# A mixture-of-experts block without a combining stage: residual rows stored early, weighted results added to them by scatters

## The reference, cut to what matters

```python
x = x + gnn(layernorm(x), edges)             # 6250 rows of 256, 200000 edges, 8 heads of 32
xt = layernorm(x)                            # input of the expert layer
probs = softmax(xt @ Wr + br)                # 8 experts
top_p, top_idx = top_k(probs, 2)
weights = top_p / top_p.sum(-1)              # the two weights of a token
xn = (xt - mean(xt)) * rsqrt(var(xt) + eps)
h = gelu((xn * ln_g[e] + ln_b[e]) @ W1[e] + b1[e])     # 256 -> 1024, for every expert e
y = h @ W2[e] + b2[e]                                  # 1024 -> 256
out = x + sum over the two chosen experts of weight * y
```

## Time and profile before

| what | us |
|---|---|
| median of 3 runs | 3188.27 (3187.75 to 3189.39) |
| the profiled execution: its own time | 3191.06 |
| the profiled execution: its span | 3189.4 |
| busy in the span: PE, DVE, ACT, POOL | 2071.1, 1937.4, 861.3, 1775.1 |

### The profile page before, as it was taken

The page is one execution under the profiler, slowest core; times in us unless marked ns, Lnnn a source line. Parts: engine busy times, 40 slices in busy tenths (PEclk is TensorE's granted clock), DMA queues, the critical chain, the costliest instruction groups (busy, mean ns, idle before and its releaser), DMA issues. The chain is left out here.

```text
span 3189.4 us, 46614 instructions
## 1 busy us (share of the span) xinstructions
PE 2071.1 (65%) x12432; PEld 1745.7 (55%) x12433; DVE 1937.4 (61%) x5386; ACT 861.3 (27%) x2271; POOL 1775.1 (56%) x1829
## 2 busy tenths in 40 slices
PE   3775666666666666666666666665342999999990
PEld 2444444444444444444444444444332999999980
DVE  6545666666666666666666666666783665656655
ACT  1222222222221112222222221111441555555540
POOL 1006777777777777777777777775475222212110
PEclk7997887878888888888878787777555999999995
DMA  1333444444444444444444444443444222212117
GB/s 44 112 110 101 109 108 108 109 108 108 109 108 108 109 108 108 109 108 108 109 108 108 109 108 108 109 108 83 136 138 137 66 79 64 86 56 73 41 43 241
DMA packets 192452, 327.35 MB, mean 103 GB/s; under 512 B 70287, under 2 KB 124542, under 8 KB 192428
## 3 DMA queue, kind: packets, MB, share of 16 engines
q0 software_dynamic: 98560, 256.53, 29.4%
q1 hardware_dynamic: 74328, 51.16, 5.7%
q10 hardware_dynamic: 19540, 19.40, 1.9%
HBM read 278.03 MB, written 47.99 MB: 102 GB/s over the span
## 5 line engine op out<-in xcount | busy, mean ns | idle before, releaser
L620 POOL DMA_INDIRECT rows<-proj_table,idx x1568 | 1486.3, 948 | 711.1 <-issue 418.2
L665 PE MATMUL banks<-weighed,onehot 128*128 128x264 f32 x3136 | 1082.8, 504 | 740.3 <-DVE weighed L736 739.5
L665 PEld LDWEIGHTS banks<-weighed,onehot 128*128 128x128 f32 x3136 | 735.5, 246 | 913.9 <-issue 767.6
L840 ACT ACTIVATE banks<-score,neg_bound 128x32 f32<-128x32 f32 x392 | 114.1, 291 | 1572.5 <-DVE score L729 1572.5
L726 DVE TENSOR_TENSOR raw_score<-rows,target 128x32 f32<-128x32 f32 x392 | 75.3, 192 | 717.4 <-DMA rows<-proj_table,idx 715.2
L736 DVE TENSOR_TENSOR weighed<-rows,banks 128x1024 f32<-128x1024 f32 x392 | 473.6, 1208 | 0.0
L1456 POOL DMA_INDIRECT results_by_token<-yrow,goes_to x104 | 108.9, 1047 | 478.6 <-DVE yrow L1404 350.4
L1343 ACT ACTIVATE hid<-banks,params 128x256 f32<-128x256 f32 x416 | 198.1, 478 | 267.7 <-PE banks L1299 261.1
L702 DVE TENSOR_TENSOR onehot<-banks,key_tab 128x512 f32<-128x512 f32 x397 | 270.1, 681 | 0.0
L1392 DVE TENSOR_TENSOR hidl<-hid,hidh 128x256 fp32r<-128x256 f32 x416 | 169.8, 424 | 149.7 <-ACT hidh L1337 149.5
L1299 PE MATMUL banks<-f_xth,w1h 128*128 128x256 f32 x832 | 236.4, 284 | 28.0 <-ACT hid L1343 14.5
(11 more groups left out here) (235 smaller groups left out, 2871.5 us busy)
## 6 DMA issues: line engine op xcount, KB each, us to landing
rows<-proj_table,idx POOLq DMA_INDIRECT x1568
w_raw<-in_L_ffn_W_dram POOLq DMA_DIRECT2D x16, 1024.0 KB, 6.3
xrow<-tokens_by_expert SPq DMA_DIRECT2D x106, 128.5 KB, 2.1
c_y<-results_by_token SPq DMA_DIRECT2D x10, 1120.0 KB
proj_table<-trow ACTq DMA_DIRECT2D x50, 128.9 KB
xin<-in_x_dram SPq DMA_DIRECT2D x50, 125.0 KB
skip_rows<-srow ACTq DMA_DIRECT2D x50, 125.0 KB
r_skin<-skip_rows SPq DMA_DIRECT2D x10, 625.0 KB
```

Source lines behind the costliest of these rows:

```text
L620: nc.gpsimd.indirect_dma_start(rows[k][:, i, :], None, table, bass.IndirectOffsetOnAxis(ap=idx[pair][:, col:col + 1], axis=0)).then_inc(ga ...
L665: mm = nc.tensor.matmul(acc_bank[u // 2 % 2][:, 0:ROW], onehot[u][:, i, :], weighed[:, k * SET + i, :], start=(u % 2 == 0 and i == 0), sto ...
```

## The change

The combining stage is dropped. While it routes, ScalarE's queue stores each chunk's x1 rows to the output. The weights are made chunk by chunk: ScalarE takes the exponential of the chunk's gaps, VectorE makes both shares and spreads them over 8 columns, one for each expert (0 where the token doesn't go). A row of `tokens_by_expert` now has 256 values, the token's number, and these 8 shares, so that one copy of a token serves both of its scatters: `second_copy` is gone. The scatters of the routing stage have 128 rows instead of 125; GpSimd first fills the 3 spare partitions with row numbers of dump rows and zeros. The loads of `r_skin` and `r_xin` are cut into parts of 112 and 13 partitions. In the expert stage VectorE copies the expert's column of shares, adds the bias into `biased`, multiplies by the share into `yrow`, and GpSimd's scatters wait for that (`y_shared`), go to the output itself, add there to what it holds, and leave out row numbers from 6250 on (padding). The diff, without declarations of semaphores and without the body of `combine_phase`:

```diff
-XROW = D + 1
+XROW = D + 1 + NX
-    xg = nc.dram_tensor("tokens_by_expert", (NX * CAP, XROW), F32).ap()
-    y2 = nc.dram_tensor("results_by_token", (2 * N + P, D), F32).ap()
+    xg = nc.dram_tensor("tokens_by_expert", (NX * CAP + P, XROW), F32).ap()
...
-            gaps=sb("gaps", [NP, NT]), warm=[sb(f"warm{k}", [P, 1]) for k in range(3)], weights=sb("weights", [NP, NT, 2]),
-            result_row=sb("result_row", [NP, NT, 2]), counts=sb("counts", [1, NX, 4], I32),
+            warm=[sb(f"warm{k}", [P, 1]) for k in range(3)],
+            result_row=sb("result_row", [NP, NT]), counts=sb("counts", [1, NX, 4], I32),
...
-        route_phase(nc, m, bank, x, skip_rows, xg)
-        expert_phase(nc, m, bank, xg, y2, ln_g, ln_b, W1, b1, W2, b2)
-        combine_phase(nc, m, y2, out)
+        route_phase(nc, m, bank, x, skip_rows, xg, out)
+        expert_phase(nc, m, bank, xg, out, ln_g, ln_b, W1, b1, W2, b2)
...
-            nc.gpsimd.iota(m["result_row"][:], [[2 * NP, NT], [1, 2]], base=0, channel_multiplier=2,
+            nc.gpsimd.iota(m["result_row"][:], [[NP, NT]], base=0, channel_multiplier=1,
...
+        SPARE = NP // 32 * 32
...
-        xn = [sb(f"r_xn{b}", [NP, C, 2, XROW]) for b in range(2)]
+        xn = [sb(f"r_xn{b}", [P, C, XROW]) for b in range(2)]
...
-        slot = [sb(f"slot{b}", [NP, C * 2], I32) for b in range(2)]
+        slot = [sb(f"slot{b}", [P, C * 2], I32) for b in range(2)]
...
+        gaps, shares, given = sb("gaps", [NP, C]), sb("shares", [NP, C, 2]), sb("given", [NP, C, 2, NX])
...
-                sp.dma_start(skin[c % 2][:], chunk(skip_rows, c)).then_inc(skin_loaded[c % 2], 16)
+                for part in NODE_PARTS:
+                    sp.dma_start(skin[c % 2][part], chunk(skip_rows, c)[part]).then_inc(skin_loaded[c % 2], 16)
...
-                sp.dma_start(xin[c % 2][:], chunk(x, c)).then_inc(xin_loaded[c % 2], 16)
+                for part in NODE_PARTS:
+                    sp.dma_start(xin[c % 2][part], chunk(x, c)[part]).then_inc(xin_loaded[c % 2], 16)
...
-                dve.wait_ge(skin_loaded[b], 16 * (c // 2 + 1))
+                dve.wait_ge(skin_loaded[b], 16 * len(NODE_PARTS) * (c // 2 + 1))
                 nc.vector.tensor_tensor(att[:], att[:], skin[b][:], ALU.add).then_inc(skin_used, 1)
+                if c == 0:
+                    dve.wait_ge(cleared, 4)
                 dve.wait_ge(skin_used, c + 1)
-                dve.wait_ge(xin_loaded[b], 16 * (c // 2 + 1))
+                dve.wait_ge(xin_loaded[b], 16 * len(NODE_PARTS) * (c // 2 + 1))
                 nc.vector.scalar_tensor_tensor(positive[:], att[:], 0.0, xin[b][:], ALU.max, ALU.add).then_inc(x_used, 1)
...
-                step(nc.vector.tensor_tensor(m["gaps"][:, of(c)], top8[:, :, 1], top8[:, :, 0], ALU.subtract))
-                dve.wait_ge(dve_step, steps[0] - 1)
+                nc.vector.tensor_tensor(gaps[:], top8[:, :, 1], top8[:, :, 0], ALU.subtract).then_inc(gaps_ready, 1)
+                settle()
                 if c:
-                    dve.wait_ge(slot_ready, 2 * c)
+                    dve.wait_ge(slot_ready, 3 * c)
...
                     dve.wait_ge(sent[b], 16 * 2 * C * (c // 2))
-                nc.vector.scalar_tensor_tensor(slot[b][:].rearrange("p (u k) -> p u k", k=2), pick[:], float(CAP), place[:],
+                nc.vector.scalar_tensor_tensor(slot[b][0:NP].rearrange("p (u k) -> p u k", k=2), pick[:], float(CAP), place[:],
                                                ALU.mult, ALU.add).then_inc(slot_ready, 1)
-                nc.vector.tensor_copy(xn[b][:, :, :, D], m["result_row"][:, of(c), :]).then_inc(slot_ready, 1)
+                dve.wait_ge(gaps_exp, c + 1)
+                step(nc.vector.tensor_scalar(shares[:, :, 1], gaps[:], 1.0, None, ALU.add))
+                settle()
+                step(nc.vector.reciprocal(shares[:, :, 0], shares[:, :, 1]))
+                settle()
+                step(nc.vector.tensor_tensor(shares[:, :, 1], shares[:, :, 0], gaps[:], ALU.mult))
+                settle()
+                step(nc.vector.tensor_tensor(given[:], one[:], shares[:].unsqueeze(3).to_broadcast([NP, C, 2, NX]), ALU.mult))
+                settle()
+                nc.vector.tensor_tensor(xn[b][0:NP, :, D + 1:XROW], given[:, :, 0, :], given[:, :, 1, :], ALU.add
+                                        ).then_inc(slot_ready, 1)
+                nc.vector.tensor_copy(xn[b][0:NP, :, D], m["result_row"][:, of(c)]).then_inc(slot_ready, 1)
...
             def second_norm(c):
                 for u in range(C):
                     t = c * C + u
-                    nc.vector.tensor_scalar(xn[c % 2][:, u, 0, 0:D], x1_of(t), mv[:, t, 0:1], rstd12[:, t:t + 1],
-                                            ALU.subtract, ALU.mult).then_inc(xn_first, 1)
+                    nc.vector.tensor_scalar(xn[c % 2][0:NP, u, 0:D], x1_of(t), mv[:, t, 0:1], rstd12[:, t:t + 1],
+                                            ALU.subtract, ALU.mult).then_inc(xn_ready, 1)
...
-            step(nc.vector.memset(padding[:, :, 0:D], 0.0))
+            step(nc.vector.memset(padding[:], 0.0))
+            settle()
             for h in range(FILL // P):
-                step(nc.vector.tensor_scalar(padding[:, h, D:XROW], m["iota_p"][:], float(2 * N), None, ALU.add))
+                step(nc.vector.tensor_scalar(padding[:, h, D:D + 1], m["iota_p"][:], float(N), None, ALU.add))
...
-            dve.wait_ge(weight_exp, 1)
-            then(nc.vector.tensor_scalar(wtmp[:], m["gaps"][:], 1.0, None, ALU.add))
-            then(nc.vector.reciprocal(m["weights"][:, :, 0], wtmp[:]))
-            then(nc.vector.tensor_tensor(m["weights"][:, :, 1], m["weights"][:, :, 0], m["gaps"][:], ALU.mult))
...
+            def gap_exponential(c):
+                act.wait_ge(gaps_ready, c + 1)
+                nc.scalar.activation(gaps[:], gaps[:], ACT.Exp).then_inc(gaps_exp, 1)
...
-            def second_copy(c):
-                act.wait_ge(xn_first, C * (c + 1))
-                nc.scalar.copy(xn[c % 2][:, :, 1, 0:D], xn[c % 2][:, :, 0, 0:D]).then_inc(xn_ready, 1)
+            def store_residual(c):
+                act.wait_ge(xn_ready, C * (c + 1))
+                rows = out[c * C * NP:(c + 1) * C * NP, :].rearrange("(u p) d -> p u d", u=C)
+                for part in NODE_PARTS:
+                    act.dma_start(rows[part], m["acc"][part, of(c), 0:D]).then_inc(x1_stored, 16)
...
             for c in range(CHUNKS):
                 if c + 1 < CHUNKS:
                     exponential(c + 1)
+                gap_exponential(c)
+                if c + 1 < CHUNKS:
                     deviations(c + 1)
-                second_copy(c)
+                store_residual(c)
                 if c + 1 < CHUNKS:
                     copy_turned(c + 1)
-            act.wait_ge(count_ready, 1)
-            nc.scalar.activation(m["gaps"][:], m["gaps"][:], ACT.Exp).then_inc(weight_exp, 1)
+            act.wait_ge(x1_stored, 16 * len(NODE_PARTS) * CHUNKS)
...
-            pe.wait_ge(slot_ready, 2 * CHUNKS)
+            pe.wait_ge(slot_ready, 3 * CHUNKS)
...
+            for b in range(2):
+                nc.gpsimd.iota(slot[b][:], [[1, 2 * C]], base=NX * CAP + (2 * b - NP * 4) * C,
+                               channel_multiplier=4 * C).then_inc(cleared, 1)
+                pool.wait_ge(cleared, 2 * b + 1)
+                nc.gpsimd.memset(xn[b][SPARE:P], 0.0).then_inc(cleared, 1)
+                pool.wait_ge(cleared, 2 * b + 2)
             for c in range(CHUNKS):
                 b = c % 2
-                pool.wait_ge(slot_ready, 2 * (c + 1))
-                pool.wait_ge(xn_ready, c + 1)
+                pool.wait_ge(slot_ready, 3 * (c + 1))
                 for u in range(C):
+                    pool.wait_ge(xn_ready, C * c + u + 1)
                     for k in range(2):
                         nc.gpsimd.indirect_dma_start(
                             xg, bass.IndirectOffsetOnAxis(ap=slot[b][:, 2 * u + k:2 * u + k + 1], axis=0),
-                            xn[b][:, u, k, :], None).then_inc(sent[b], 16)
+                            xn[b][:, u, :], None).then_inc(sent[b], 16)
...
-        goes_next = sb("goes_next", [P, HALF])
+        goes_next, share, biased = sb("goes_next", [P, HALF, 1 + NX]), sb("share", [P, HALF]), sb("biased", [P, HALF, D])
...
-                    nc.vector.tensor_copy(goes_next[:, h:h + 1], xrow[:, h, D:XROW])
+                    nc.vector.tensor_copy(goes_next[:, h, :], xrow[:, h, D:XROW])
...
                     dve.wait_ge(stored[h], 16 * g)
-                    nc.vector.tensor_copy(goes_to[h][:], goes_next[:, h:h + 1]).then_inc(goes_ready[h], 1)
+                    nc.vector.tensor_copy(goes_to[h][:], goes_next[:, h, 0:1]).then_inc(goes_ready[h], 1)
+                nc.vector.tensor_copy(share[:].unsqueeze(2), goes_next[:, :, bass.ds(expert_of + 1, 1)]).then_inc(share_ready, 1)
                 for h in range(HALF):
                     dve.wait_ge(goes_ready[h], g + 1)
```

(40 more changed lines are left out.)

47 lines of the change are left out of this document (removed).

## The result

The change made the kernel slower: 3207.81 us in the median of 4 runs (3206.93 to 3212.63) against 3188.01 (3187.60 to 3189.39), a ratio of 1.0063 with a 95% interval of 1.0051 to 1.0075. The prediction had said 3162 us, faster. The profiled execution took 3207.91 us, with a span of 3205.9.

The account below looks back on a forecast made before the run. TensorE was taken to pace the expert stage, with the combining stage alone on the path. Combining -78.1, routing +5, splits +3 and scatter costs in the tiles summed to -26 us: median 3162 us, range 3120 to 3270.

Parts of the forecast that it names:

- part 3: Expert stage: what an accumulating scatter costs over a plain one, bounded by 0 and 2.4 us, taken as 0.75.
- the term a: Expert stage: extra time of one accumulating scatter over a plain one, taken as 0.75 us; the sum is zero at 1.03.
- the two bounds of the text: Accumulating scatter: 0 extra if landing stays covered; 2.4 us if a whole 1.9 us read precedes and issue grows by half.
- rival B: Expert stage: adding scatters' landing sets the pace, goes_to waiting, from 1.1 us extra per scatter; 3231 to 3314 us; chance 0.32.
- The rule on two reads: Adding scatter: only doubled read traffic costs, 0.31 us per scatter, whole sum -60 us.
- the gather row: Traced gather of 128 rows, 0.94 us to issue, data used 1.9 us behind the issue; taken as sign of read latency.
- The loop: Expert tile: yrow, two scatters and landings, goes_to, normalization, next yrow; 10.03 us beside TensorE's 11.71, 1.68 us of cover.
- The period formula: Expert tile: second chain 10.03 + 0.9 = 10.93 us + 2a, leaving 0.78 us of cover for 2a.
- The sum: Whole kernel: -64.7 + 14a + 39 max(0, 2a - 0.78), giving -26 us with a = 0.75.
- The combining term: End of the kernel: 82.6 us from last scatter to span's end become 4.5, saving 78.1 us less 2a.
- Routing: Routing stage: +10 us for 1.0 us more in each of ten chunks, -5 from faster first loads, net +5.
- rival C: Routing stage: ScalarE's stores block like the 125-partition loads, up to 46 us over ten chunks, 3208 us; chance 0.06.

Follow-up runs that it names:

- Experiment 1: Changed kernel with scatters that overwrite instead of adding, row check kept; 3119.60 us, ratio 0.9778 to the kernel before.
- experiment 4: Changed kernel with goes_to and share filled after the next tile's normalization, from a copy of goes_next; 3121.80 us, ratio 0.9781 to the kernel before.
- experiment 5: Changed kernel whose second scatter of a tile no longer waits for the first's landing; 3116.86 us, ratio 0.9765 to the kernel before.
- experiment 3: Changed kernel with bias times share formed during the wait, then one operation per half for yrow; 3178.77 us, ratio 0.9962 to the kernel before.

## Why the prediction was wrong

**The step that failed** is part 3, the term a: "0.44 + 0.31 = 0.75: this is what I take, nearer to the scatter row, because reads and writes of different rows overlap in one transfer." Experiment 1 against the kernel after gives a = 3.8 - 2.4 = 1.4 us, between the two bounds of the text (0 and 2.4) but beyond 1.1, the point from which rival B was said to decide. The part that was put at nothing is GpSimd's issue. It grew from 0.99 to 1.555 us, 0.57 more; the text named such a growth for the upper bound and left it out of the value without a reason. With it the value would have been 1.32 us, and the forecast would have been rival B's.

The rest of a, some 0.8 us, lies in the transfer itself. The busy share of the 16 DMA engines in 40 slices of 0.1 us from the start of one scatter's issue on (in tenths), and what its queue moved in these 4 us (packets, MB, share of 16 engines), first in the kernel after, then in experiment 1:

```profile
DMA  0000000000000000000009954696989852000000
q0 software_dynamic: 144, 0.13, 30.0%
```

```profile
DMA  0000000000000007999100000000000000000000
q0 software_dynamic: 48, 0.13, 9.4%
```

The adding transfer begins 2.1 us behind the start of the issue instead of 1.5: that is the longer issue, and no other wait ahead of the transfer shows. It then lasts 1.3 us instead of some 0.45. The same 0.13 MB go in 144 packets instead of 48, and they keep the engines busy for 30.0% of 4 us, 1.20 us, instead of 0.38. So the reason given for the low value, reads and writes that overlap in one transfer, didn't hold the cost down. How the longer transfer divides between reading the old rows and moving smaller packets stays open: no run separates the two.

That 0.75 lies near the 0.8 us measured behind the issue is luck, for it was added up from a latency ahead of the transfer, which doesn't show, and 0.31 us for bytes. Both terms were also misread: 2.84 - 2.46 is 0.38 and not 0.44, and the 0.32 MB of the earlier trace rows are nearly two and a half scatters of 0.13 MB and not three, so that one took 0.38 us and not 0.31.

**The rule on two reads.** It gave a = 0.31, from bytes, and the text set it against the latency that the gather row shows. Neither is what the traces show: of the 1.4 us, 0.57 are issue, and the engine time of the transfer grew threefold, from 0.38 to 1.20 us, and not twofold, as the text's 0.31 for a second reading has it. Bandwidth over the stage was far from short (57 GB/s). The records of an adding scatter hold the same 0.13 MB as those of a plain one, so this figure leaves out any reading of old rows; that would be 0.26 MB in a tile of 13.74 us, some 19 GB/s more (an estimate). The Trainium skill (Collectives: The Full Stack, section on the bandwidth ceiling) states of the add in a ReduceScatter that it is slow for its second source read and not for its arithmetic. No run here shows that traffic; as a price for one transfer that somebody waits for, the rule was too low in this case.

**The loop was right.** Of the four pieces, those without a landing were predicted as 1.98 and 3.23 us and measured as 1.93 and 3.21; the two landings hold all of the miss. The period formula, 10.93 + 2a, gives 13.73 for a = 1.4, and 13.74 was measured; a is known to a tenth only, so an agreement to the hundredth is chance. The text's sign for B was `goes_to` waiting in nearly every tile, which came true, and a period of 13.9 and more, which was set too high: with the a = 1.1 from which B was to decide, the same formula gives 13.13. So B is what happened, with the mechanism and at the place that it named; experiments 4 and 5 show it by removing the loop in two ways at unchanged issue and landing.

**The sum.** The formula with a = 1.4 gives -64.7 + 19.6 + 39 x 2.02 = +34 us; the spans of the two profiled executions differ by 16.5 (3205.9 - 3189.4). Term by term:

| term | formula, a = 1.4 | measured |
|---|---|---|
| combining, from the last bias addition to the span's end | -75.3 | -73.0 (87.1 to 14.1) |
| expert stage, first to last bias addition | +104.0 | +93.1 (614.8 to 707.9) |
| routing, first load to the weights' load | +5 | +1.8 (214.2 to 216.1) |
| start of routing | 0 | -5.2 (2229.53 to 2224.31) |

The rest, -0.2, lies between routing and the first tile. In the expert stage 38 steady periods paid 1.96 us each in the mean, where the formula has 39 at 2.02; the six behind a weight load paid 2.4 to 3.3 us instead of 3.7 (their periods are 14.1 to 15.0); the seven with a split of weights paid 1.3 us in all instead of 3. The combining term was sound but for its ending: the span ends 7.4 us behind the last scatter's issue at 3198.50, of which 3.8 are a landing, and not some 5, since the text took 1.3 us for what follows the landing.

**Routing** was mis-sized by some 3 us. Two rows each of SyncE's queue and VectorE in order of time, of the kernel after:

```profile
2224.31 0.90 SPq L939 DMA_DIRECT2D r_skin<-skip_rows  x2
...
2418.81 13.38 SPq L949 DMA_DIRECT2D tokens_by_expert<-padding  x8
```

```profile
2232.59 1.49 DVE L982 SCALAR_TENSOR_TENSOR positive<-att,r_xin 125x1280 f32<-125x1280 f32 x1 [1.27 <-DMA r_xin<-in_x_dram]
...
2293.18 1.70 DVE L1008 TENSOR_SCALAR xl<-acc,r_mv,rstd 125x256 f32<-125x256 f32 x5
```

The first use of `r_xin` comes 8.3 us behind the first load instead of 14.0, the 5.7 that the text read from the earlier trace rows. The chunk of VectorE grew from 17.15 to 17.82 us, 0.67 and not 1.0; from the third chunk on the five-fold normalization, as at 2293.18, is shorter than before (1.70 against 1.88 to 2.09 us), which the text hadn't foreseen and no run explains. As predicted, GpSimd now waits for VectorE (58.9 us) and padding still ends the stage; rival C is out, for ScalarE's stores were issued in 0.418 us in the median, and the stage as a whole grew by 1.8 us. That C's 3208 us is the measured time to the microsecond is chance.

**Open.** Routing began 5.2 us earlier in the profiled execution after. Over the profiled executions of all runs it began between 2221.3 and 2230.3 us with the change and between 2229.5 and 2232.4 without. Those that began earliest were also faster than their own medians (3111.18 against 3116.86 us in experiment 5), so part of this is spread between executions; that some us of it belong to the change, whose table of row numbers is smaller, wasn't tested.

## What to carry to other kernels

An accumulating scatter is dear first for whoever waits for its landing (1.4 us more here); it also kept the DMA engines busy three times as long as a plain one (1.20 against 0.38 us), for which there was room here, with engines busy for 0.30 of the stage. Before results are added in DRAM, find who waits for the landing, count how many landings lie one behind another in a tile's loop, and compare the loop with the pace of the busiest engine. Here removing a stage of 76 us lost 20 us as it stood. Two operations of VectorE fewer in the loop made that a gain of 12 us (experiment 3); opening the loop made it 69 to 75 us, by ordering only what must be ordered (experiment 5) or by putting the wait behind work (experiment 4); either alone was enough. When a cost is unknown, and the answer turns on it at 1.03 us with bounds of 0 and 2.4, the value in the lower half needs a reason for each of its parts, the issue too.

## What the runs showed of the hardware

GpSimd needs 1.555 us to issue an adding scatter of 128 rows of 1 KB and 0.986 us for the same scatter without the addition; the check of row numbers costs nothing that can be seen (1.559 without it, with the addition). The adding scatter moves in 144 packets and keeps the 16 DMA engines busy for 1.20 us in the mean, the plain one in 48 packets and for 0.38 us. A scatter of 128 rows of 265 values in the routing stage is issued in 0.976 us in the median, where one of 125 rows of 257 values took 1.187 in the kernel before: fewer and shorter rows were dearer.
